# Edge loop of a four-layer graph network: one scatter product split into four, each on 32 columns of the array

## The chip, the cores and the metric

The kernel runs on one core of one Trainium2 chip. The metric is device time in microseconds (us) from launch to end; lower is better. A core has a matrix engine (TensorE, PE in the profile, with its weight loads listed apart as PEld), a vector engine (VectorE, DVE), a scalar engine (ScalarE, ACT), GpSimd (POOL) and SyncE (SP). Each runs its own list of instructions, and they wait for one another by semaphores. TensorE multiplies weights that were loaded into its array beforehand with a stream of columns, and adds the results up in PSUM, 8 banks of 128 partitions by 512 fp32 values.

## What is computed

Four graph layers one after the other on 1250 nodes with 512 features, each followed by a residual sum and a layer norm. The change lies in the second, a message layer over 21,250 edges. Cut to what matters:

```python
def _L1_gnn_ref(node_feats, edge_attrs, edge_feats, edge_index, ...):
    x0, x1 = _lin_irreps(x0, x1, W_up0, W_up1)
    h = edge_feats
    for W in (W_mlp1, W_mlp2, W_mlp3):
        h = SILU_2MOM * silu(h @ W / sqrt(W.shape[0]))
    w1, w2, w3, w4 = split(h @ W_mlp4 / sqrt(W_mlp4.shape[0]), 4)
    s0, s1 = x0[sender], x1[sender]
    y0, y1 = edge_attrs[:, 0:1], edge_attrs[:, 1:4]
    p1 = w1 * s0 * y0
    p2 = (w2 * s0)[:, :, None] * y1[:, None, :]
    p3 = w3[:, :, None] * s1 * y0[:, None, :]
    p4 = w4 * einsum('eum,em->eu', s1, y1) / SQRT3
    msg0 = segment_sum(concatenate([p1, p4], -1), receiver, 1250)
    msg1 = segment_sum(concatenate([p2, p3], 1), receiver, 1250)
    o0, o1 = _lin_irreps(msg0, msg1, W_out0, W_out1)
```

The two segment sums are what the changed product computes: for each edge 1024 message values are added to the row of its destination node.

## The kernel before

The edges have been sorted by destination into blocks of 125 nodes and padded. That gives G = 52 groups of 512 edges, each with destinations in one block only. The edge loop takes a group in GT = 4 steps of 128 edges, so it has 208 steps. It is written by hand for each engine, with two groups (`par` 0 and 1) to a turn of the hardware loop at L859.

For a step `k` the engines do this:

- TensorE, `tpw` (L847, L848): the last layer of the edge network, two products in the fp32r type of 128 x 512 into one of four banks (`tpw_bank`). The loop issues it three steps ahead of the step that it scatters.
- VectorE, `products` (L1604 to L1614): the messages `prod[:, k, :]`, 128 edges by 1152 values, and at L1606 `sel[:, k, :]`, the 128 x 125 matrix that holds a one where an edge's destination is that node. L1606 waits until the scatter four steps back is done (`s_scat_done`), since it overwrites its buffer.
- ScalarE: `first_term` (L1188), `times_y` (L1195 three times, then L1196, which makes `sely` out of `sel` by one of the edge's factors and lets the scatter go by `s_y_ok`).
- TensorE, `scat` (L852): two fp32 products with 128 edges as the contraction. The weights are the 125 columns of `sely` or `sel`, the stream is 512 columns of `prod`, and the result adds up over the four steps in two banks of PSUM, 125 partitions each. The banks alternate between the two groups, 2 and 3 or 4 and 5.

After each group VectorE adds the two banks into `acc` (`add_sums`, L1621) and prepares the low half of the hidden rows of a later group (`split_hidden`, L1627, after ScalarE's L1178). GpSimd fetches the sender rows of the group after next with four gathers (L597), after its copies L591 and L592, as soon as the group that used their buffers is read.

TensorE's list in the loop is strictly `tpw` three steps ahead, then `scat` of this step, then the next pair.

Of the kernel before, what the change touches and what calls it, by code (L numbers as in the profile page):

```python
# [10 lines left out]
NP, NB = 125, 10  # L11
KT = D // 128
EC = E // NP
GT = 4
# [51 lines left out]
def build(nc, a, out):  # L66
# [7 lines left out]
    with ctx:  # L74
# [39 lines left out]
        def at(off, shape, dt=f32):  # L114

            size = int(np.prod(shape[1:]))
            words = size if dt in (f32, f32r, i32, u32) else (size + 1) // 2
            assert off + words <= ARENA
            v = arena[:shape[0], off:off + words]
            if dt != f32:  # L120
                v = v.bitcast(dt)
            if len(shape) == 3:
                v = v.rearrange("p (a b) -> p a b", a=shape[1])
            if len(shape) == 4:
                v = v.rearrange("p (a b c) -> p a b c", a=shape[1], b=shape[2])
            return v

        PS = ctx.enter_context(nc.psum_tensor("PS", [128, 8, 512], f32))
# [81 lines left out]
        prod = at(14336, [128, GT, 9 * MUL])  # L210
# [411 lines left out]
        def _(pe):  # L622
            t = nc.tensor
# [123 lines left out]
            for b in range(NB):  # L747
# [3 lines left out]
                for j in range(NB):  # L751
                    ins = t.transpose(PS[:NP, 3 * (b % 2) + j // 4, (j % 4) * NP:(j % 4 + 1) * NP],
                                      cnt_f[:, b % 2, j * NP:(j + 1) * NP], ident[:NP, :NP])
# [38 lines left out]
            with pe.Fori(0, H // 2) as i:  # L792
                for par in range(2):
                    pe.wait_ge(s_hs_ok, i * 2 + (par + 1))
                    pe.wait_ge(s_head_free, i * 2 + (par + 1))
                    for sblk in range(NB):
                        pe.wait_ge(s_p_ok, i * (2 * NB) + (par * NB + sblk + 1))
                        for q in range(3):
                            n0, n1 = q * 512, min(N, (q + 1) * 512)
                            ins = t.matmul(PS[:, 3 * par + q, 0:n1 - n0], hs[:, sblk, par * C:par * C + 2 * C],  # L800
                                           wt[:, sblk % WR, n0:n1], start=(sblk == 0), stop=(sblk == NB - 1))
# [47 lines left out]

            def scat(par, k):  # L850
                for q, w in enumerate((sely, sel)):
                    ins = t.matmul(PS[:NP, 2 + 2 * par + q, :], w[:, k, :], prod[:, k, q * 512:(q + 1) * 512],  # L852
                                   start=(k == 0), stop=(k == GT - 1))
                ins.then_inc(s_scat_done, 1)
            pe.wait_ge(s_w4_ok, 2)
            pe.wait_ge(s_h3_ok, 1)
# [2 lines left out]
            with pe.Fori(0, G // 2) as i:  # L859
                for par in range(2):  # L860
                    pe.wait_ge(s_gsum_ok, i * 2 + (par + 1))
                    for k in range(GT):

                        if k == 1:
                            pe.wait_ge(s_h3_ok, i * 2 + (par + 2))
                        tpw((k + GT - 1) % GT, par if k == 0 else 1 - par)
                        pe.wait_ge(s_prod_ok, i * 8 + (4 * par + k + 1 + GT))
                        pe.wait_ge(s_y_ok, i * 8 + (4 * par + k + 1))
                        scat(par, k)
# [20 lines left out]
            for b in range(NB):  # L890
# [5 lines left out]
                for q in range(4):  # L896
                    pair = ((0, w_o0[:, 0, :]), (7, w_o0[:, 1, :])) if q == 0 else \
                           ((3 + q, w_o1[:, 0, :]), (q, w_o1[:, 1, :]))
                    for n, (c, w) in enumerate(pair):
                        ins = t.matmul(PS[:NP, 4 + b % 2, q * MUL:(q + 1) * MUL], msgT[:, b % 2, c * NP:(c + 1) * NP], w,  # L900
                                       start=(n == 0), stop=(n == 1))
# [16 lines left out]
            def agg_part(w, b0, k):  # L918

                for q in range(3):  # L920
                    n0, n1 = q * 512, min(N, (q + 1) * 512)
                    ins = t.matmul(PS[:, b0 + q, 0:n1 - n0], w, P50[:, k, n0:n1], start=(k == 0), stop=(k == NB - 1))  # L922
                return ins

            def x_feat(k, f):
                return x_sb[:, k, f * 128:(f + 1) * 128]

            for k in range(NB):
                pe.wait_ge(s_p2_ok, k + 1)
                for f in range(2):  # L930
                    ins = agg_part(x_feat(k, f), 3 * f, k)
# [10 lines left out]
            for q in range(3):  # L942
                n0, n1 = q * 512, min(N, (q + 1) * 512)
                ins = t.matmul(PS[:, q, 0:n1 - n0], ones[:NP, 0:128], Psum[:, n0:n1], start=True, stop=True)
# [29 lines left out]
            for b in range(NB + 1):  # L974
                if b < NB:
# [3 lines left out]
                    for k in range(KT):  # L979
                        ins = t.transpose(PS[:, 7, k * 128:k * 128 + NP], x_sb[:, b, k * 128:(k + 1) * 128], ident[:NP, :NP])  # L980
                    ins.then_inc(s_xt3_ps, 1)
                if b >= 1:
# [6 lines left out]
                    for k in range(KT):  # L989
                        ins = t.matmul(PS[:NP, 5 + c % 2, :], xT3[:, k, c * NP:(c + 1) * NP], w_l3[:, KT + k, :],  # L990
                                       start=(k == 0), stop=(k == KT - 1))
                    ins.then_inc(s_z_ps, 1)
            pe.wait_ge(s_z_cp, NB)
            for b in range(NB):
# [4 lines left out]
                for k in range(NB):  # L999
                    if b == 0:  # L1000
                        pe.wait_ge(s_p3_ok, k + 1)
                    ins = t.matmul(PS[:NP, b % 2, :], cnt50[:, k, b * NP:(b + 1) * NP], z_sb[:, k, :],  # L1002
                                   start=(k == 0), stop=(k == NB - 1))
# [784 lines left out]
```

## Time and profile before

| what | value |
|---|---|
| median of 3 runs | 2041.71 us (2039.19 to 2046.14) |
| profiled execution, its time | 2038.94 us |
| profiled execution, its span | 2036.9 us |
| granted TensorE clock, mean | 0.93 |
| busy over the whole span: PE, DVE, ACT | 83%, 79%, 44% |
| edge loop, first `tpw` to last `scat` | 872.4 to 1364.9 us, 492.5 us |

The span is the time from the first to the last instruction; what lies around it was 2.0 us in this execution. A step of the edge loop on TensorE is one row pair L847 and L848 and four records of L852 in the timeline. Each of the two fp32 products of `scat` appears as two weight loads and two matmuls, hence 832 records for 416 products. In the timeline the matmuls overlap on paper, since their ends are modelled with the way through the array. What tells the rate is the distance between starts.

### The profile page before, as it was taken

The numbers are of one execution on the slowest core, as the hardware profiler recorded it, in microseconds if no ns is written. First come the engines' busy times: TensorE is split into PE (matmuls) and PEld (weight loads), VectorE is DVE, ScalarE is ACT, GpSimd is POOL, SyncE is SP. The second block draws the span as 40 slices with busy tenths as digits, with TensorE's granted clock in tenths as the row PEclk, the third lists the DMA queues.
The fourth block names the chain that finished last, engine by engine and source line by source line (L and its number), as shares of the span: only waits on it lengthen the run. The fifth ranks groups of instructions, "written<-read, shape, count | busy, mean of one in ns | idle before, by whom it ended". The sixth has DMA issues, their size and how long they took to land.

```text
span 2036.9 us, 21846 instructions
## 1 busy us (share of the span) xinstructions
PE 1693.8 (83%) x5296; PEld 870.4 (43%) x5296; DVE 1607.7 (79%) x3252; ACT 895.4 (44%) x1833; POOL 527.2 (26%) x597
## 2 busy tenths in 40 slices
PE   2668888788387777479999999999598998999997
PEld 1445545533133333444444444457353443444443
DVE  9997899889899999789999999987665754762222
ACT  0112555666355454457777777763204423441100
POOL 4777870044000000045455555520000000002000
PEclk9788999988698899789999999998799999999999
DMA  5101000123210010154545454530010111111000
GB/s 166 10 6 8 6 5 1 36 101 110 103 39 35 32 42 0 56 150 140 151 135 155 133 154 136 153 74 1 25 42 21 62 62 62 58 56 52 0 25 25
DMA packets 66428, 133.78 MB, mean 66 GB/s; under 512 B 19156, under 2 KB 22752, under 8 KB 66385
## 3 DMA queue, kind: packets, MB, share of 16 engines
q1 hardware_dynamic: 40561, 70.33, 11.1%
q0 software_dynamic: 22080, 56.10, 10.3%
q10 hardware_dynamic: 3744, 6.82, 0.9%
q8 instruction: 22, 0.36, 0.1%
q14 instruction: 21, 0.17, 0.0%
HBM read 117.78 MB, written 15.24 MB: 65 GB/s over the span
## 4 chain that ended last, share of the span: by engine, by line
DVE 39%; PE 38%; issue 15%; DMA 4%; DVEq 3%; ACT 2%; SPq 0%; POOL 0%; ACTq 0%; POOLq 0%
PE PS L954 15%; DVE arena L1492 5%; PE PS L922 4%; PE PS L1002 4%; DVE arena L1608 4%; PE PS L738 3%; DVE arena L1488 3%; DVE arena L1353 3%; DVE arena L1604 3%; DVE arena L1611 2%; DVE arena L1614 2%; DVE arena L1352 2%; DVE arena L1383 2%; PE PS L998 2%; PE PS L990 2%
## 5 line engine op out<-in xcount | busy, mean ns | idle before, releaser
L852 PE MATMUL PS<-arena 128*125 128x512 f32 x832 | 397.1, 600 | 20.4 <-ACT arena L1196 20.3
L954 PE MATMUL PS<-arena 128*125 128x512 f32 x720 | 314.5, 600 | 12.2 <-ACT arena L1262 6.6
L1195 ACT ACTIVATE arena<-arena,gslot 128x128 f32<-128x128 f32 x624 | 204.4, 390 | 136.6 <-DVE arena L1608 129.0
L800 PE MATMUL PS<-arena 125*128 125x512 f32 (+1 forms) x480 | 196.3, 552 | 79.0 <-DVE arena L1492 78.9
L597 POOL DMA_INDIRECT arena<-xup,gidx x208 | 218.1, 1048 | 88.4 <-issue 50.0
L561 POOL DMA_INDIRECT recs<-arena x170 | 211.1, 1242 | 62.1 <-issue 47.7
L852 PEld LDWEIGHTS PS<-arena 128*125 128x125 f32 x832 | 152.2, 188 | 157.5 <-issue 101.3
L954 PEld LDWEIGHTS PS<-arena 128*125 128x125 f32 x720 | 136.8, 190 | 189.3 <-issue 189.3
L847 PE MATMUL PS<-w4r,h3r 128*128 128x512 f32 x211 | 168.2, 797 | 10.3 <-DVE h3r L1627 10.3
L800 PEld LDWEIGHTS PS<-arena 125*128 125x128 f32 x480 | 90.3, 199 | 185.1 <-DVE arena L1492 102.4
L1148 ACT ACTIVATE arena<-arena,c 125x1250 f32<-125x1250 f32 x80 | 107.0, 1337 | 137.6 <-DVE arena L1488 137.4
L738 PE MATMUL PS<-arena 128*125 128x512 bf16 (+1 forms) x624 | 128.5, 361 | 38.0 <-DVE arena L1383 37.8
L1488 DVE SCALAR_TENSOR_TENSOR arena<-arena,c 125x1250 f32<-125x1250 f32 x90 | 136.0, 1514 | 19.3 <-DMA arena<-uv_rows 17.1
L618 POOL CAST arena<-cnt_s 125x1250 f32<-125x1250 uint16 x10 | 12.6, 1303 | 513.7 <-PE PS L954 513.7
L591 POOL COPY gidx<-gld 128x4 uint32<-128x4 uint32 x52 | 9.7, 187 | 494.9 <-DMA gld<-recs 348.5
L1452 DVE CUSTOM_DVE_ANT_0 arena<-arena 125x1250 bf16<-125x1250 bf16 x80 | 111.2, 1454 | 10.1 <-DMA arena<-as_rows 7.8
L738 PEld LDWEIGHTS PS<-arena 128*125 128x125 bf16 x624 | 81.5, 145 | 88.0 <-DVE arena L1383 48.1
L1383 DVE TENSOR_SCALAR arena<-iota_src,pslot 128x1250 bf16<-128x1250 f16 x208 | 116.6, 581 | 0.0
L1492 DVE SCALAR_TENSOR_TENSOR arena<-arena,cnt_s 125x1250 f32<-125x1250 f32 x80 | 116.0, 1453 | 0.0
L1612 DVE TENSOR_TENSOR arena<-PS,arena 128x384 f32<-128x384 f32 x208 | 113.5, 546 | 0.0
L922 PE MATMUL PS<-arena,x_sb 125*128 125x512 f32 (+1 forms) x240 | 86.1, 520 | 19.3 <-DVE arena L1492 19.3
L771 PE MATMUL PS<-arena,w_m 16*128 16x512 f32 (+1 forms) x156 | 87.5, 690 | 17.5 <-ACT arena L1112 17.3
(235 smaller groups left out, 2905.9 us busy)
## 6 DMA issues: line engine op xcount, KB each, us to landing
arena<-in_spline_wT SPq DMA_DIRECT2D x16, 1024.0 KB, 5.3
arena<-h_rows SPq DMA_DIRECT2D x104, 128.0 KB, 3.4
arena<-uv_rows SPq DMA_DIRECT2D x18, 610.4 KB
h_rows<-arena ACTq DMA_DIRECT2D x26, 256.0 KB, 2.1
arena<-as_rows SPq DMA_DIRECT2D x8, 610.4 KB
arena<-xup,gidx POOLq DMA_INDIRECT x208, 4.2
recs<-arena POOLq DMA_INDIRECT x170, 2.6
x_sb<-in_x SPq DMA_DIRECT2D x1, 2500.0 KB
```

The source lines that it names most:

```text
L561: pool.indirect_dma_start(out=recs, out_offset=bass.IndirectOffsetOnAxis(stage_pos[:, sl, k:k + 1], 0), in_=stage_rec[:, sl, k, :], in_off ...
L597: pool.indirect_dma_start(out=ring[:, par * GT + k, :], out_offset=None, in_=xup, in_offset=bass.IndirectOffsetOnAxis(gidx[:, par, k:k + 1 ...
L738: ins = t.matmul(PS[:NP, 3 * par + q, 0:n1 - n0], oh_dst[:, par * GT + k, 0:NP], oh_src[:, par * GT + k, n0:n1], start=(k == 0), stop=(k = ...
L800: ins = t.matmul(PS[:, 3 * par + q, 0:n1 - n0], hs[:, sblk, par * C:par * C + 2 * C], wt[:, sblk % WR, n0:n1], start=(sblk == 0), stop=(sb ...
L847: t.matmul(PS[:, tpw_bank[k], :], h3r[:, par, cols], w4r[:, 0, :], start=True, stop=False)
L852: ins = t.matmul(PS[:NP, 2 + 2 * par + q, :], w[:, k, :], prod[:, k, q * 512:(q + 1) * 512], start=(k == 0), stop=(k == GT - 1))
L922: ins = t.matmul(PS[:, b0 + q, 0:n1 - n0], w, P50[:, k, n0:n1], start=(k == 0), stop=(k == NB - 1))
L954: ins = t.matmul(PS[:NP, b, :], basis[:, slot, (k * HB + b) * NP:(k * HB + b + 1) * NP], w_sp[:, slot, k * D:(k + 1) * D], start=(first an ...
L1195: A(pr[:, 4 + m, :], pr[:, 8, :], ACT.Copy, scale=y[:, 1 + m:2 + m])
L1383: ins = v.tensor_scalar(oh_src[:, par * GT + k, :], iota_src[:], pslot[:, par, k:k + 1], None, ALU.is_equal)
L1488: v.scalar_tensor_tensor(dst, U, cc, V, ALU.add, ALU.max).then_inc(ok, 1)
L1492: v.scalar_tensor_tensor(dst, e, 1.0, cm, ALU.min, ALU.mult).then_inc(ok, 1)
```

## The change

In `scat` the one product per half of the message becomes four. The first takes destination columns 0 to 31 of `sely` or `sel` as weights, the second 32 to 63, the third 64 to 95, the fourth 96 to 124, which is 29. Each names the 32 columns of the array that it is to use (`tile_position=(0, c0)`) and writes the 32 PSUM partitions of the same numbers. All four stream the same 128 x 512 block of `prod`. The semaphore is still raised once, by the last product. Nothing else is changed.

```diff
             def scat(par, k):
                 for q, w in enumerate((sely, sel)):
-                    ins = t.matmul(PS[:NP, 2 + 2 * par + q, :], w[:, k, :], prod[:, k, q * 512:(q + 1) * 512],
-                                   start=(k == 0), stop=(k == GT - 1))
+                    for c0 in range(0, NP, 32):
+                        c1 = min(NP, c0 + 32)
+                        ins = t.matmul(PS[c0:c1, 2 + 2 * par + q, :], w[:, k, c0:c1], prod[:, k, q * 512:(q + 1) * 512],
+                                       start=(k == 0), stop=(k == GT - 1), tile_position=(0, c0))
                 ins.then_inc(s_scat_done, 1)
```

TensorE's list around the first step of the loop, before: L847 and L848 are `tpw`, L852 is `scat`, the rest is the arithmetic of loop counters.

```order
405 L847 MATMUL PS<-w4r,h3r 128x512
406 L848 MATMUL PS<-w4r,h3r 128x512
407 L867 ISA
408 L868 REGISTER_ALU
409 L852 MATMUL PS<-arena 125x512 x2
```

The same list in the changed kernel, where the lines have moved by two, and `scat` is L854:

```order
409 L854 MATMUL PS<-arena 32x512 x3
410 L854 MATMUL PS<-arena 29x512
411 L854 MATMUL PS<-arena 32x512 x3
412 L854 MATMUL PS<-arena 29x512
413 L867 REGISTER_ALU
414 L847 MATMUL PS<-w4r,h3r 128x512
415 L848 MATMUL PS<-w4r,h3r 128x512
```

Two products between one `tpw` and the next have become eight, with the four that belong to one half of the message in a row; no instruction changes its place against another, and the lists of the other engines are as they were.

## Rows read from the trace of the kernel before

**Rows 1.** The page: busy time of the engines, share and instructions.

```profile
PE 1693.8 (83%) x5296; PEld 870.4 (43%) x5296; DVE 1607.7 (79%) x3252; ACT 895.4 (44%) x1833; POOL 527.2 (26%) x597
```

**Rows 2.** Busy us (instructions) by engine in the edge loop, granted clock, DMA.

```profile
core 0: us, PE busy (x) PEld busy (x) DVE busy (x) ACT busy (x) POOL busy (x), PEclk, DMA share, GB/s
872.00:1364.90 492.90, 472.10 (x1254) 233.58 (x1254) 459.73 (x1351) 346.95 (x1091) 243.94 (x310) 0.99 0.50 141
```

**Rows 3.** The chain that ended last, 1099 to 1109 us: shares by line.

```profile
by line: issue 22.9%; DVE arena L1608 19.7%; DVE arena L1611 13.0%; DVE arena L1604 12.1%; DVE arena L1614 10.3%; DVE h3r L1627 6.9%; DVE arena L1606 4.7%; DVE arena L1612 4.7%; DVEq L1617 3.5%; DVEq L1610 1.6%; DVEq L1603 0.8%; DVE arena L
```

**Rows 4.** L1627 in 1092 to 1113 us: count, ns min/median/max, first and last start.

```profile
L1627 DVE TENSOR_TENSOR h3r<-arena,h3r x3: 689/690/690, 1094.3 to 1112.9; 64x512 fp32r<-64x512 f32 x3
```

**Rows 5.** Timeline of PE: start us, us, what, count, [idle before <-releaser].

```profile
1100.68 1.95 PE L852 MATMUL PS<-arena 128*125 128x512 f32 x4 [0.41 <-ACT arena L1196]
1102.07 0.80 PE L847 MATMUL PS<-w4r,h3r 128*128 128x512 f32 x1
1102.70 0.39 PE L848 MATMUL PS<-w4r,h3r 128*128 128x512 f32 x1
1102.93 1.88 PE L852 MATMUL PS<-arena 128*125 128x512 f32 x4
1104.25 0.80 PE L847 MATMUL PS<-w4r,h3r 128*128 128x512 f32 x1
...
1108.62 0.79 PE L847 MATMUL PS<-w4r,h3r 128*128 128x512 f32 x1
```

**Rows 6.** Timeline of the weight loads of the same step.

```profile
1103.36 0.19 PEld L852 LDWEIGHTS PS<-arena 128*125 128x125 f32 x1 [0.24 <-issue]
1103.79 0.19 PEld L852 LDWEIGHTS PS<-arena 128*125 128x125 f32 x1 [0.24 <-issue]
1104.22 0.19 PEld L847 LDWEIGHTS PS<-w4r,h3r 128*128 128x128 f32 x1 [0.24 <-issue]
```

**Rows 7.** Waits in 880 to 1365 us: in total, times, longest.

```profile
POOL gidx L591 <- ACT arena L1196: 146.3, 50, 5.9
ACT arena L1195 <- DVE arena L1608: 129.0, 102, 4.0
...
PE PS L852 <- ACT arena L1196: 20.3, 48, 5.0
...
DVE arena L1621 <- PE PS L852: 2.6, 1, 2.6
```

**Rows 8.** Weight loads of L706, fp32 with 16 weight columns, one after another.

```profile
166.44 0.10 PEld L706 LDWEIGHTS PS<-arena,wa 128*16 128x16 f32 x1 [0.33 <-issue]
...
169.02 0.10 PEld L706 LDWEIGHTS PS<-arena,wa 128*16 128x16 f32 x1 [0.33 <-issue]
```

**Rows 9.** Engines' busy us and granted clock (sixth value) in the stretch of L706.

```profile
166.00:171.00 5.00, 5.00 (x17) 1.45 (x16) 2.95 (x5) 0.59 (x1) 3.80 (x5) 1.00 0.09 5
```

**Rows 10.** Timeline of PE from L706 (16 weight columns) to L658 (125).

```profile
170.02 1.11 PE L706 MATMUL PS<-arena,wa 128*16 128x226 f32 x5
171.07 1.15 PE L658 MATMUL PS<-wa,arena 128*125 128x16 f32 x9
```

**Rows 11.** The last of these by itself, its start and modelled length.

```profile
170.79 0.35 PE L706 MATMUL PS<-arena,wa 128*16 128x226 f32 x1
```

**Rows 12.** Timeline of PE at the start of the edge loop.

```profile
873.40 0.63 PE L847 MATMUL PS<-w4r,h3r 128*128 128x512 f32 x1
873.83 0.63 PE L848 MATMUL PS<-w4r,h3r 128*128 128x512 f32 x1
```

**Rows 13.** Engines' busy us and granted clock (sixth value) there.

```profile
873.00:876.00 3.00, 3.00 (x8) 1.96 (x6) 0.00 (x0) 0.00 (x0) 2.39 (x3) 0.53 0.56 178
```

**Rows 14.** The end of the loop: the last sum waits for the last scatter.

```profile
1365.05 1.22 DVE L1621 TENSOR_TENSOR arena<-PS,arena 125x1024 f32 x1 [3.12 <-PE PS L852]
```

## The prediction

> **What bounds the kernel now.** The page first: TensorE is busy for 83% of the span and VectorE for 79% [rows 1], a mean over stages that says nothing of this edit. So I read the stage it touches. In the edge loop TensorE is busy for 472 and VectorE for 460 of 493 us [rows 2], so two engines are nearly full. The chain of waits tells which of them sets the pace. It runs through VectorE's lines L1604 to L1627, with VectorE's own issue time between them, and the lines of `scat` and `tpw` are not in it [rows 3]. The list of waits agrees: TensorE waits for ScalarE (20.3 us, the end of a chain that starts on VectorE), and VectorE waited for a scatter only once, 2.6 us [rows 7]. The period of a group is VectorE's: L1627 comes once a group, and 1094.3 to 1112.9 are two periods, so 9.30 us, or 52 x 9.30 = 484 us for the loop [rows 4].
>
> TensorE's own need comes from the starts of its matmuls. When nothing holds it up a step takes 1104.25 - 1102.07 = 2.18 us [rows 5]. The weight loads inside `scat` start 0.43 us apart, 1103.36 and 1103.79 [rows 6], and there are four records to a step, two for each fp32 product. So `scat` streams for 4 x 0.43 = 1.72 us, and `tpw` takes the other 0.46 us. A group needs 4 x 2.18 = 8.72 us of TensorE. **The slack is 0.58 us a group**, 0.15 us a step. That is all that this edit may add before TensorE is the bound.
>
> **What the change removes and adds.** It removes 4 records of L852 a step and adds 16: eight products, each with two weight loads and two matmuls, if the split is as for all fp32 products here. The edit takes nothing from another engine. What one of the 16 costs is in the trace. L706 is an fp32 product with 16 weight columns; of its loads the first shown and the seventh start at 166.44 and 169.02, so 2.58 / 6 = 0.43 us apart [rows 8]. **A narrow product streams its 512 columns as slowly as a wide one.** What gets shorter is the weight load, 0.10 us against 0.19 [rows 6, 8], and that lies under the running matmul. Everything then hangs on how many of the 16 run at once, which no row shows, since no product of this kernel stands on other columns of the array than the first. The bounds, per step:
>
> - All in a row: 16 x 0.43 = 6.88 us.
> - Four at once throughout: 16 / 4 x 0.43 = 1.72 us, what `scat` takes now. Below it nothing is to be had: the 4 instructions of each tile must still stream one after another.
> - Between them, overlap only where neighbours in the list differ in tile. The list holds the two halves of one fp32 product next to each other, and both need the same 32 columns of the array. If matmuls start in the order of the list, the second half waits 0.43 us for the first, and the next tile's first half can start only behind it. The first half of each product then runs beside the second half of the one before. Eight products take 8 + 1 = 9 slots: 9 x 0.43 = 3.87 us.
>
> I take the last. The starts in the timeline follow the list everywhere that I looked [rows 5], and loads run ahead of a matmul by one slot and no further [rows 6], so I expect an engine that looks one step ahead, not one that sorts its work by tile.
>
> The Trainium skill, "TensorE: Matmul & The Clock Gate", section "Packing small matmuls — row/col tiling", says that matmuls on different tiles run at the same time, with four nanoseconds or so added per tile, and also that matmuls start and end strictly in program order. No run here shows either so far. Its sum for a pack counts one matmul per tile; an fp32 product has two. By its first sentence alone the result would be the second bound, by both together the third.
>
> **The switches.** Twice a step the array goes from its whole width to 32 columns and back. The trace has such a switch: L706 has 16 weight columns, L658 has 125. The last L706 starts at 170.79 [rows 11] and the first L658 at 171.07 [rows 10], 0.28 us; the L706 of that size start (170.79 - 170.02) / 4 = 0.19 us apart. So it costs 0.09 us; I take 0.1. The upper bound is the whole tail of the last matmul, 0.35 - 0.19 = 0.16 us [rows 11], and an uncovered wide load of 0.19 us [rows 6], 0.35 us together; the lower bound is nothing. The Trainium skill, "TensorEngine Tiling (Array Packing)", section "Key Properties", speaks against the change here: a change of tiling mode drains the engine. By the row a drain costs 0.1 us. Had the page meant the whole tail, the sum would be by the upper bound.
>
> **The sum.** Step: 3.87 (scatter) + 0.46 (`tpw`) + 2 x 0.1 (switches) = 4.53 us. Group: 18.1 us against VectorE's 9.30, so TensorE is the bound by far, and nothing covers the rest. VectorE, ScalarE and GpSimd then wait: `sel` and `prod` are kept for four steps and the sums alternate banks, so TensorE has its next operands in time. Loop: 208 x 4.53 = 942 us in place of 484, so **+458 us**. The start of the loop (before the first scatter) does not change. The tail, where L1621 waits 3.1 us for the last scatter [rows 14], grows by the 2.15 us that one scatter grows by, which the sum has in it. Span: 2036.9 + 458 = 2495 us. The median of the runs lies 4.8 us above the span of the profiled execution (2.8 above its own time, 2038.94), so I predict 2500 us.
>
> **The bounds of this case.** Switches at nothing: 4.33 x 208 = 901, so +417 and 2459 us. Switches at 0.35: 5.03 x 208 = 1046, so +562 and 2604. If half of the eight narrow loads that follow a load of the same tile are no longer covered, 4 x 0.10 x 208 = 83 us more, 2687.
>
> **Rivals.**
>
> 2. *All in a row.* The tiles share one stream. Step: 6.88 + 0.46 + 0.2 = 7.54 us, loop 1568, +1084, so 3126 us. For it: every narrow product in the trace is as long as a wide one [rows 8]. Against it: those all stand on the same columns, so they could not overlap.
> 3. *Faster.* The scatter ends sooner than 1.72 us, because the tiles' streams overlap even between the two halves. VectorE's 9.30 us remain the bound, and what TensorE can give back is what VectorE waits for it: 2.6 us in the loop [rows 7] and 3.1 at its end [rows 14], 6 us, so 2036. If all time in which VectorE isn't busy were such waits, it would be 493 - 460 = 33 us and 2009. It decides from a step below 2.18 us. Against it: rows 8 give no narrow matmul below 0.43 us.
> 4. *The clock.* At the start of the loop the granted clock is 0.53 in the mean, so mostly the lower level of 1.2 GHz, after TensorE sat idle, and an fp32r matmul there takes 0.43 us [rows 12, 13] instead of some 0.23. With all at the lower level the forecast's step is 2 x 4.33 + 0.2 = 8.86 us and the time about 3400. Against it: narrow matmuls in a row kept a granted clock of 1.00 [rows 9], and TensorE would be busier than before.
>
> **How the numbers follow.** Forecast 0.45, four at once 0.35, in a row 0.14, clock or another overlap 0.04, faster 0.02. The likeliest gives 2500, by itself 2459 to 2687. The range takes in the first two cases, 2048 to 2690, and leaves out in a row, the clock and faster: 0.2. A measurement of this kernel can tell about 0.3%, 6 us, from no change. Of the case of four at once a tenth may lie within that, so 0.04 for same; faster 0.02; slower 0.94.
>
> **What would show it.** In the profile after, the edge loop should take 950 us, its matmuls should come in starts 0.43 us apart with two records at each, and a step should be 4.5 us. VectorE's busy share in the loop should fall from 93% to about half, and the chain should run through TensorE. If the loads of the eight products start in fours within 0.1 us and a step is below 3 us, it is rival 1; if all 16 stand 0.43 apart, rival 2. The forecast is wrong if an fp32 product of 32 columns is not made of two halves, or if its halves do not stand side by side in what TensorE gets.

## The result, and the profile after

The changed kernel takes 2084.04 us (median of 4 runs, 2080.22 to 2086.16) against 2042.51 us (4 runs) for the kernel before: ratio 1.0201, 95% interval 1.0176 to 1.0226, 41.5 us slower. I had forecast 2500 us. The direction was right and the time lies inside the range, but the size was off by a factor of eleven: 458 us of loss forecast, 41.5 measured. What came is the first rival, four tiles at once throughout (2053 to 2157 us, most likely 2065). So the slower time does not bear out the forecast: its way to a loss, a scatter of 3.87 us, isn't there, and what makes the kernel slower is another term.

The page of the changed kernel, busy time by engine and the chain that ended last:

```profile
PE 1752.1 (84%) x7792; PEld 787.5 (38%) x7792; DVE 1608.7 (77%) x3252; ACT 895.4 (43%) x1833; POOL 526.5 (25%) x597
...
PE 60%; DVE 24%; issue 9%; DMA 4%; ACT 2%; DVEq 1%; SPq 0%; POOL 0%; ACTq 0%; POOLq 0%
```

Against [rows 1] TensorE has 2496 more matmul records, 12 for each of 208 steps, as forecast, and only 58 us more busy time. The edge loop from the first `tpw` to the last `scat` (busy us and records of PE, PEld, DVE, ACT, POOL, then the granted clock), and the shares by line of the chain in 1109 to 1119 us:

```profile
878.40:1411.90 533.50, 528.07 (x3750) 148.62 (x3750) 458.46 (x1350) 346.77 (x1090) 243.60 (x310) 0.99 0.46 130
```

```profile
by line: PE PS L854 73.9%; PE PS L847 17.1%; PE PS L848 9.4%
```

The loop takes 533.5 us in place of 492.5: the whole loss, 41.0 us, is in it. VectorE does the same work in it, 458 us against 460 [rows 2], and the chain, which ran through VectorE alone [rows 3], now runs through TensorE alone. (The loop starts 6 us later in this execution. The edit has no part ahead of it, and the medians differ by 41.5 us, so I give that no cause; executions of the kernel before lie up to 7 us apart.)

The timeline of PE in the steady loop (start us, us, what, how many records), which answers to [rows 5]:

```profile
1120.28 0.50 PE L847 MATMUL PS<-w4r,h3r 128*128 128x512 f32 x1
1120.61 0.40 PE L848 MATMUL PS<-w4r,h3r 128*128 128x512 f32 x1
1120.94 1.92 PE L854 MATMUL PS<-arena 128*32 128x512 f32 x16
1122.79 0.50 PE L847 MATMUL PS<-w4r,h3r 128*128 128x512 f32 x1
...
1130.33 0.50 PE L847 MATMUL PS<-w4r,h3r 128*128 128x512 f32 x1
```

Sixteen records stand in 1.85 us, from 1120.94 to the next `tpw` at 1122.79. One record alone streams for 0.43 us, so 16 in a row would be 6.88. The weight loads of the same stretch, which answer to [rows 6]:

```profile
1120.93 0.15 PEld L854 LDWEIGHTS PS<-arena 128*32 128x32 f32 x8 [0.36 <-issue]
1121.39 0.12 PEld L854 LDWEIGHTS PS<-arena 128*32 128x32 f32 x4 [0.30 <-issue]
1121.82 0.12 PEld L854 LDWEIGHTS PS<-arena 128*32 128x32 f32 x4 [0.30 <-issue]
1122.79 0.19 PEld L847 LDWEIGHTS PS<-w4r,h3r 128*128 128x128 f32 x1 [0.84 <-issue]
```

Eight loads go at once, two for each tile (one to work with, one ahead), then four and four at distances of 0.43 to 0.46 us. That is the sign that I had named for rival 1. All four tiles stream side by side, and a tile's second half does not hold up the next tile. Four records of 0.43 us to a tile are 1.72 us, as before.

So `scat` costs what it did, and the loss lies at its edges. A step is (1130.33 - 1120.28) / 4 = 2.51 us, 0.33 more than 2.18. From `scat` to `tpw` it is 1.85 us instead of 1.72, 0.13 more; from `tpw` to `scat` 1120.94 - 1120.28 = 0.66 instead of 0.46, 0.20 more.

These two pieces are not the two directions, since the first load after a change falls into the piece behind it. The rows allow a finer split. The second round of narrow loads comes 1121.39 - 1120.93 = 0.46 us after the first, and the third 0.43 after that: 0.03 us are the first narrow load, which no running matmul covers. The other 0.10 of the 0.13 pass between the end of the last narrow record and the load of L847. Then L847 starts 0.33 us ahead of L848, and L848 0.33 ahead of `scat`, where a product of this kind takes 0.23 between wide neighbours (shown below in the run on the slack). The first 0.10 is the wide load of L847, now uncovered (the next load starts 0.10 behind it); the second passes between the end of L848 and the narrow loads. So, by this reading of starts, each change of shape has a pause of 0.10 us and behind it a first load that nothing covers: 0.10 + 0.03 = 0.13 us from wide to narrow, 0.10 + 0.10 = 0.20 from narrow back to wide.

The load of L847 shows the change of shape. In [rows 6] it starts 0.24 us after the load before it ends, under a running matmul. Here the load engine stands idle for 0.84 us and starts at 1122.79, with the matmul record that it belongs to. A group now takes 1130.33 - 1120.28 = 10.05 us of TensorE against 9.30 of VectorE, and 52 x 0.75 = 39 us of the 41 follow. The list of waits in 880 to 1405 us (in total, times, longest) has what answers to the last two lines of [rows 7]:

```profile
DVE arena L1623 <- PE PS L854: 60.8, 51, 3.2
...
PE PS L854 <- ACT arena L1198: 5.4, 1, 5.4
```

VectorE's sum at the end of a group waited once for a scatter before; now it waits in 51 of 52 groups, 1.2 us each. TensorE's 48 waits for ScalarE, 20.3 us, have shrunk to one of 5.4 us.

### The profile page after: what moved, and what is told of

It reads as the page before. It is cut to its first block, busy times and chain, and to the rows that moved or that the text cites. A ratio compares the mean times of both kernels' runs of the same rounds, so it can differ in the third digit from the quotient of the medians.

```text
span 2084.0 us, 26838 instructions
## 1 busy us (share of the span) xinstructions
PE 1752.1 (84%) x7792; PEld 787.5 (38%) x7792; DVE 1608.7 (77%) x3252; ACT 895.4 (43%) x1833; POOL 526.5 (25%) x597
## 4 chain that ended last, share of the span: by engine, by line
PE 60%; DVE 24%; issue 9%; DMA 4%; ACT 2%; DVEq 1%; SPq 0%; POOL 0%; ACTq 0%; POOLq 0%
PE PS L854 19%; PE PS L956 15%; DVE arena L1494 5%; PE PS L847 4%; PE PS L924 4%; PE PS L1004 4%; DVE arena L1355 3%; DVE arena L1490 3%; PE PS L738 3%; PE PS L848 2%; DVE arena L1385 2%; DVE arena L1354 2%; PE PS L1000 2%; PE PS L992 2%; DVE arena L1506 2%
## 5 line engine op out<-in xcount | busy, mean ns | idle before, releaser
L854 PE MATMUL PS<-arena 128*32 128x512 f32 (+1 forms) x3328 | 401.5, 600 | 5.4 <-ACT arena L1198 5.4
L956 PE MATMUL PS<-arena 128*125 128x512 f32 x720 | 314.4, 600 | 12.2 <-ACT arena L1264 6.6
L956 PEld LDWEIGHTS PS<-arena 128*125 128x125 f32 x720 | 136.8, 190 | 189.3 <-issue 189.3
L854 PEld LDWEIGHTS PS<-arena 128*32 128x32 f32 (+1 forms) x3328 | 84.4, 109 | 208.5 <-issue 192.7
L1623 DVE TENSOR_TENSOR arena<-PS,arena 125x1024 f32 x52 | 63.7, 1224 | 66.2 <-PE PS L854 66.2
L847 PE MATMUL PS<-w4r,h3r 128*128 128x512 f32 x211 | 105.8, 501 | 10.2 <-DVE h3r L1629 10.2
L847 PEld LDWEIGHTS PS<-w4r,h3r 128*128 128x128 f32 x211 | 39.9, 189 | 185.5 <-issue 185.2
```

Of the source, the lines that this page charges most:

```text
L847: t.matmul(PS[:, tpw_bank[k], :], h3r[:, par, cols], w4r[:, 0, :], start=True, stop=False)
L854: ins = t.matmul(PS[c0:c1, 2 + 2 * par + q, :], w[:, k, c0:c1], prod[:, k, q * 512:(q + 1) * 512], start=(k == 0), stop=(k == GT - 1), til ...
L956: ins = t.matmul(PS[:NP, b, :], basis[:, slot, (k * HB + b) * NP:(k * HB + b + 1) * NP], w_sp[:, slot, k * D:(k + 1) * D], start=(first an ...
```

## Experiments

Two theories after the result. **Shape**: the tiles cost nothing, and going to the narrow shape and back costs 0.33 us of TensorE a step, of which VectorE's pace had hidden 0.15. **Record**: each of the 12 more records costs 0.0275 us of issue, which is also 0.33. The runs also test whether the tiles overlap fully, and how far the engine sees ahead. Differences below are each against the kernel before as it ran beside them.

**One tile of the four.**

```diff
-                    for c0 in range(0, NP, 32):
+                    for c0 in (0,):
```

> Only the product on the first 32 columns is left, so the sums of the other 93 destination nodes of a block are left out. Four matmul records a step instead of 16, all on one tile. If the four tiles of the changed kernel run fully beside one another and the extra 0.33 us of a step is the price of going to the narrow shape and back, a step stays at 2.51 us and the time at 2084 us. If the 0.33 us is paid per record (12 more records, 0.0275 us each), the step is back at 2.18 us, VectorE is the bound again and the time is 2042 us. If the tiles overlap only in part, the step falls below 2.4 us, and the time below 2070 us.

Measured: 2080.49 us against 2044.27, ratio 1.0186 (1.0169 to 1.0203), 36 us slower.

```profile
1121.50 1.90 PE L854 MATMUL PS<-arena 128*32 128x512 f32 x4
1123.33 0.50 PE L847 MATMUL PS<-w4r,h3r 128*128 128x512 f32 x1
...
1125.83 0.50 PE L847 MATMUL PS<-w4r,h3r 128*128 128x512 f32 x1
```

With a quarter of the records the scatter still takes 1123.33 - 1121.50 = 1.83 us and the step 2.50. So the other three tiles are almost free: 0.02 us a step, or the 4 to 5 us between 36 and 41.5. The record theory, which wanted 2042 us, is out.

**The tiles one by one.**

```diff
-                for q, w in enumerate((sely, sel)):
-                    for c0 in range(0, NP, 32):
-                        c1 = min(NP, c0 + 32)
+                for c0 in range(0, NP, 32):
+                    c1 = min(NP, c0 + 32)
+                    for q, w in enumerate((sely, sel)):
```

> The same eight products a step, in another order: both halves of the message on the first 32 columns, then both on the next, and so on. Four matmul records in a row now want the same tile. If each tile has a line of its own for at least four waiting instructions, nothing changes: step 2.51 us, 2084 us. If the engine starts matmuls in the order of the list (what the prediction took), the step is over 4.5 us and the time over 2500 us. If it looks ahead by two records only, a tile blocks for 0.86 us before the next one starts: 3 x 0.86 us more a step, 2.6 us, and the time is over 2600 us.

Measured: 2088.0 us against 2044.27, ratio 1.0221 (1.0204 to 1.0239). The weight loads:

```profile
1121.64 0.17 PEld L854 LDWEIGHTS PS<-arena 128*32 128x32 f32 x8 [0.36 <-issue]
1122.09 0.15 PEld L854 LDWEIGHTS PS<-arena 128*32 128x32 f32 x4 [0.28 <-issue]
1122.52 0.15 PEld L854 LDWEIGHTS PS<-arena 128*32 128x32 f32 x4 [0.28 <-issue]
```

Four records in a row want the same tile here, and still eight loads go first and then four and four. Whose they are can be told by shape, since the fourth tile alone has 29 columns. The first eight loads by shape (1121.64 to 1121.82 us), and the matmuls that run in 1121.72 to 1121.82:

```profile
L854 PEld LDWEIGHTS PS<-arena 128*32 128x32 f32 x6 | 0.2, 108 | 0.4 <-issue 0.4
L854 PEld LDWEIGHTS PS<-arena 128*29 128x29 f32 x2 | 0.1, 106 | 0.0
```

```profile
L854 PE MATMUL PS<-arena 128*32 128x512 f32 x3 | 0.6, 617 | 0.0
L854 PE MATMUL PS<-arena 128*29 128x512 f32 x1 | 0.6, 615 | 0.0
```

In the order of the list the fourth tile's records are the last four of the sixteen. Two of its loads are among the first eight, and one of its matmuls runs among the first four. So a record that waits for its tile does not stop those behind it, at least 12 records deep (the fourth tile's first is the thirteenth). Whether each tile has a queue of its own or one queue is searched, the times can't tell. The step is 2.53 us instead of 2.51.

**Two tiles of 64 columns.**

```diff
-                    for c0 in range(0, NP, 32):
-                        c1 = min(NP, c0 + 32)
+                    for c0 in range(0, NP, 64):
+                        c1 = min(NP, c0 + 64)
```

> Two products on 64 and 61 columns in place of four on 32: 8 matmul records a step. If the price is that of the change of shape, twice a step, it is there in full: step 2.51 us, 2084 us. If it is paid per record, 4 more records cost 0.11 us, less than TensorE's slack of 0.15 us, and the time is 2042 to 2046 us.

Measured: 2086.75 us, ratio 1.0211 (1.0191 to 1.023).

```profile
1121.96 0.50 PE L847 MATMUL PS<-w4r,h3r 128*128 128x512 f32 x1
1122.30 0.40 PE L848 MATMUL PS<-w4r,h3r 128*128 128x512 f32 x1
1122.62 1.94 PE L854 MATMUL PS<-arena 128*64 128x512 f32 x8
1124.49 0.50 PE L847 MATMUL PS<-w4r,h3r 128*128 128x512 f32 x1
```

Half the records, and the same price: step 2.53 us, with the same 0.66 us ahead of the scatter. The price is that of leaving the wide shape and coming back, the same for 64 columns as for 32.

**Every second step.**

```diff
+                    wd = 32 if k % 2 else 128
-                    for c0 in range(0, NP, 32):
-                        c1 = min(NP, c0 + 32)
+                    for c0 in range(0, NP, wd):
+                        c1 = min(NP, c0 + wd)
```

> The four narrow products only in steps 1 and 3 of a group, the one wide product in steps 0 and 2. If the loss comes from 0.33 us in each changed step, a group needs 2 x 2.18 + 2 x 2.51 = 9.38 us of TensorE against VectorE's 9.30, so some 4 us more than before plus what two nearly equal engines lose to one another: 2044 to 2058 us. If the loss were in proportion to the changed steps, it would be half of 41 us: 2063 us.

Measured: 2050.03 us against 2044.27, ratio 1.0028 (1.0015 to 1.0041), 5.8 us.

```profile
1120.95 0.50 PE L847 MATMUL PS<-w4r,h3r 128*128 128x512 f32 x1
...
1125.66 0.50 PE L847 MATMUL PS<-w4r,h3r 128*128 128x512 f32 x1
```

Two steps take 4.71 us and a group 9.42, so 52 x 0.12 = 6 us. Half the changes of shape cost a seventh of the loss, since most of them fit into TensorE's slack.

**The slack by itself, without tiles.** The kernel before, with one short product more in each step:

```diff
+                t.matmul(PS[:, tpw_bank[k], :], h3r[:, par, cols], w4r[:, 1, :], start=False, stop=False)
                 t.matmul(PS[:, tpw_bank[k], :], h3r[:, par, cols], w4r[:, 1, :], start=False, stop=True).then_inc(s_tpw_ps, 1)
```

> The kernel before, all wide, with the second product of tpw (L848) issued twice, so that the message weights are off in their low part: 0.22 us more of TensorE a step, no tiles. It tests the slack of 0.15 us a step. Step 2.40 us, group 9.60 us against 9.30: 208 x 2.40 - 484 = 15 us more, and some more from two nearly equal engines: 2057 to 2070 us. If the slack is larger than 0.22 us, 2043 us.

Measured: 2061.12 us against 2041.03, ratio 1.0097 (1.0076 to 1.0117), 20 us.

```profile
1120.92 0.79 PE L847 MATMUL PS<-w4r,h3r 128*128 128x512 f32 x1
1121.56 0.40 PE L848 MATMUL PS<-w4r,h3r 128*128 128x512 f32 x1
1121.79 0.39 PE L849 MATMUL PS<-w4r,h3r 128*128 128x512 f32 x1
1122.02 1.88 PE L853 MATMUL PS<-arena 128*125 128x512 f32 x4
1123.34 0.79 PE L847 MATMUL PS<-w4r,h3r 128*128 128x512 f32 x1
```

The step is 2.42 us here, and one short product between wide neighbours takes 0.23 (L848, L849 and L853 start 0.23 apart). 0.23 us more of TensorE's time a step cost 20 us, where 208 x 0.23 = 48 would be due without slack. The rule "52 x (TensorE's group - 9.30)" gives 18 to 20 us for this run, 6 for the one with every second step (5.8 measured) and 39 for the change (41.5 measured). The 2 us or so that are left may be what two nearly equal engines lose to each other; no run shows it.

**A loop without a change of shape.** To have `tpw` on column tiles too I replaced its two fp32r products by one fp32 product of the same rows. That is slower, so three kernels: all wide, only the scatter narrow, both narrow.

```diff
-                t.matmul(PS[:, tpw_bank[k], :], h3r[:, par, cols], w4r[:, 0, :], start=True, stop=False)
-                t.matmul(PS[:, tpw_bank[k], :], h3r[:, par, cols], w4r[:, 1, :], start=False, stop=True).then_inc(s_tpw_ps, 1)
+                for c0 in range(0, 128, 32):
+                    ins = t.matmul(PS[c0:c0 + 32, tpw_bank[k], :], h3r[:, par, k * 128 + c0:k * 128 + c0 + 32].bitcast(f32), w_m4,
+                                   start=True, stop=True, tile_position=(0, c0))
+                ins.then_inc(s_tpw_ps, 1)
```

The diff is that of the third; the first two have one product in place of the loop.

> The scatter as before, wide. The two fp32r products of tpw are replaced by one fp32 product of the same rows with the unrounded weights, which can be split into column tiles. All wide, no change of shape. It is the base for the next two. Two records at 0.43 us in place of 0.46 us: step 1.72 + 0.86 = 2.58 us, TensorE is the bound, 208 x 2.58 - 484 = 53 us more than before: 2097 us.

> The same fp32 tpw, wide, with the scatter of the changed kernel: two changes of shape a step. If a pair of them costs 0.33 us whatever stands on either side: step 2.91 us, 605 - 484 = 121 us more than before: 2165 us, 69 us above the all-wide one. If the 0.33 us belonged to the fp32r products (a short product after which nothing covers a load), it would be 2097 to 2110 us.

> The fp32 tpw too in four products on 32 columns, so that the whole loop stays in one shape: 24 records a step, none wide. If the loss comes from the changes of shape, it is gone: step 2.58 us, 2097 us, as with all wide. If narrow tiles cost something of their own (more records, the end of a pack), it stays at 2.8 us or more and 2140 us or more.

Measured against 2041.03 us: all wide 2095.1 (ratio 1.0261, 1.0232 to 1.0289), scatter narrow 2162.25 (1.0598, 1.0571 to 1.0625), both narrow 2096.17 (1.0274, 1.0253 to 1.0295). The timeline of the second, then of the third:

```profile
1121.40 1.92 PE L853 MATMUL PS<-arena 128*32 128x512 f32 x16
1123.25 1.13 PE L847 MATMUL PS<-arena,h3r 128*128 128x512 f32 x2
1124.31 1.92 PE L853 MATMUL PS<-arena 128*32 128x512 f32 x16
```

```profile
1119.68 1.90 PE L856 MATMUL PS<-arena 128*32 128x512 f32 x16
1121.40 1.04 PE L848 MATMUL PS<-arena,h3r 128*32 128x512 f32 x8
1122.26 1.90 PE L856 MATMUL PS<-arena 128*32 128x512 f32 x16
```

This decides it. With two changes of shape a step is 1124.31 - 1121.40 = 2.91 us, with none 1122.26 - 1119.68 = 2.58, in the kernel with nothing but narrow products, the same as with nothing but wide ones to 1 us of the whole time. The price is 67 us / 208 = 0.32 us a step. The two pieces are those of the changed kernel: 1123.25 - 1121.40 = 1.85 in place of 1.72 from `scat` to `tpw`, 1124.31 - 1123.25 = 1.06 in place of 0.86 from `tpw` to `scat`. It has nothing to do with the fp32r type.

**Scatters in pairs.** The changed kernel, with the changes of shape halved by order alone:

```diff
-                    for k in range(GT):
-                        if k == 1:
-                            pe.wait_ge(s_h3_ok, i * 2 + (par + 2))
+                    for k in (0, 2):
                         tpw((k + GT - 1) % GT, par if k == 0 else 1 - par)
+                        if k == 0:
+                            pe.wait_ge(s_h3_ok, i * 2 + (par + 2))
                         pe.wait_ge(s_prod_ok, i * 8 + (4 * par + k + 1 + GT))
+                        tpw(k, 1 - par)
                         pe.wait_ge(s_y_ok, i * 8 + (4 * par + k + 1))
                         scat(par, k)
+                        pe.wait_ge(s_prod_ok, i * 8 + (4 * par + k + 2 + GT))
+                        pe.wait_ge(s_y_ok, i * 8 + (4 * par + k + 2))
+                        scat(par, k + 1)
```

> The changed kernel with TensorE's list in pairs: tpw of two steps, then the narrow scatters of two steps, so one change of shape and back for two steps. Saved against the changed kernel: 2 x 0.33 = 0.66 us a group, so 9.38 us and 2050 us, if nothing else waits. The second tpw of a pair now needs the hidden rows of the next group right after the first step of this one, 0.7 us or so of TensorE's time a group: 10.1 us and 2085 us at most. Below 2075 us it says that the price is one of the changes of shape; at 2084 us or above it says nothing.

Measured: 2047.52 us against 2041.09, ratio 1.0027 (1.0014 to 1.004). Of the 41.5 us 35 are back, with all 3328 narrow records in place.

```profile
1119.91 0.50 PE L847 MATMUL PS<-w4r,h3r 128*128 128x512 f32 x1
...
1121.05 3.64 PE L854 MATMUL PS<-arena 128*32 128x512 f32 x32
1124.61 0.50 PE L847 MATMUL PS<-w4r,h3r 128*128 128x512 f32 x1
```

Two steps take 4.70 us, a group 9.40: TensorE and VectorE are level. The wait for the hidden rows, which I feared, doesn't show.

**Is VectorE the bound of the kernel before?** Then taking work off it must gain. L1627 (0.69 us a group) goes to GpSimd, at first in the kernel before and in the changed one as it stands:

```diff
-                        if k == 0:
-                            split_hidden(1 - par, i * 2 + (4 - par))
...
+            def split_low(par, n, n_gath):
+                for k in range(GT):
+                    pool.wait_ge(s_gath[(1 - par) * GT + k], n_gath)
+                pool.wait_ge(s_h3hi_ok, n)
+                pool.nop(nofuse=True)
+                pool.tensor_tensor(h3r[HID:128, par, :], h3[HID:128, par, :], h3r[HID:128, par, :].bitcast(f32), ALU.subtract)\
+                    .then_inc(s_h3_ok, 1)
...
```

> The kernel before, all wide, with the 50 subtractions of L1627 in the loop (0.69 us each) moved from VectorE to GpSimd, ahead of the gathers of the same group. If VectorE's 9.30 us a group is what bounds the kernel before, and TensorE comes next with 8.72 us, the group falls to 8.72 to 8.9 us: 52 x 0.4 to 0.58 us less, 2012 to 2022 us. If GpSimd's later gathers become the wait, or VectorE was not the bound, 2035 to 2045 us.

> The same move in the changed kernel. There TensorE needs 10.05 us a group, so relief for VectorE should bring nothing: 2080 to 2085 us. If the two engines slow each other down (the loss of the change is partly VectorE's), it falls below 2075 us.

Measured: 2099.1 us (ratio 1.0285, 1.0271 to 1.0299) and 2096.41 us (1.0268, 1.0252 to 1.0283) against 2041.09. Both missed what I expected. The waits of the first in 900 to 1350 us:

```profile
POOL h3r L610 <- DMA arena<-xup,gidx: 106.8, 34, 4.3
ACT arena L1201 <- DMA arena<-xup,gidx: 103.0, 43, 3.5
```

In this form GpSimd waits until its own gathers have landed (the loop over `s_gath`) before it subtracts, 3.1 us each time. The next gathers start that much later, and ScalarE waits for them. A new wait took the place of the old bound, and the two runs say nothing on the question. Nearly equal times with wide and narrow scatters show only that TensorE did not bound these two.

The same again without that wait, and in the kernel before alone. Into a second buffer ScalarE writes zero for rows 0 to 63 and the rounded values for rows 64 to 127, and GpSimd subtracts that buffer over all 128 partitions. So one operation makes rows 0 to 63 and the low halves in rows 64 to 127.

```diff
-                A(h3r[:, par, :], h3[:, par, :], ACT.Copy).then_inc(s_h3hi_ok, 1)
+                A(h3m[:, par, :], h3[:, par, :], ACT.Copy, scale=low[:, 0:1]).then_inc(s_h3hi_ok, 1)
...
+                pool.wait_ge(s_h3hi_ok, n)
+                pool.nop(nofuse=True)
+                pool.tensor_tensor(h3r[:, par, :], h3[:, par, :], h3m[:, par, :].bitcast(f32), ALU.subtract)\
+                    .then_inc(s_h3_ok, 1)
...
```

> Again the kernel before, all wide, with the subtractions of L1627 on GpSimd, but in a form over all 128 partitions (ScalarE writes zero over the upper 64 rows), so that GpSimd need not wait until its earlier gathers have landed, which cost 107 us of waiting in the run before this one. VectorE then needs some 8.6 us a group, TensorE 8.72. If VectorE's 9.30 us bounded the kernel before and the gathers, 1.1 us later than before, are still in time: 52 x 0.3 to 0.58 us less, 2012 to 2026 us. If the gathers are late by their new delay: 2040 to 2060 us.

Measured: 2030.6 us against 2043.62, ratio 0.9939 (0.9924 to 0.9955), 13 us faster than the kernel before, which the changed one trails by 41.5 us. That is less than the 16 us (52 x 0.3) at least that I had named. Its L611 (count, ns min/median/max, first and last start):

```profile
L611 POOL TENSOR_TENSOR h3r<-arena x3: 1272/1282/1282, 1107.5 to 1125.6; 128x512 fp32r<-128x512 f32 x3
```

The group takes (1125.6 - 1107.5) / 2 = 9.05 us instead of 9.30, and 52 x 0.25 = 13 us. Work taken off VectorE gains, which together with the chain in [rows 3] and the run on the slack says that VectorE was the bound before. TensorE's 8.72 us is not reached, and the trace says why. The chain in 1110 to 1128 us, by line, then VectorE's L1616 (L1604 in the kernel before) without and with GpSimd's subtraction beside it:

```profile
by line: issue 24.4%; DVE arena L1616 18.2%; DVE arena L1620 18.0%; DVE arena L1623 11.5%; DVE arena L1626 10.8%; DVEq L1629 5.5%; DVE arena L1618 5.1%; DVE arena L1624 4.1%; DVEq L1622 1.6%; DVE arena L1633 0.9%; DVEq L1645 0.7%; DVEq L163
```

```profile
1124.37 0.34 DVE L1616 SCALAR_TENSOR_TENSOR arena<-arena,gslot 128x128 f32<-128x128 f32 x1
...
1125.60 1.28 POOL L611 TENSOR_TENSOR h3r<-arena 128x512 fp32r<-128x512 f32 x1 [1.78 <-ACT arena L1190]
...
1126.08 0.95 DVE L1616 SCALAR_TENSOR_TENSOR arena<-arena,gslot 128x128 f32<-128x128 f32 x1
```

The chain still runs through VectorE. Once a group its L1616 takes 0.95 us in place of 0.34 while L611 runs; over the loop L1616 takes 494 ns in the mean, against 341 for L1604 in the kernel before. That is 4 x 0.153 = 0.61 us a group, most of the 0.69 that had been taken off. So the move relieved VectorE far less than its expectation reckoned. That the group is shorter by 0.25 us and not by the 0.08 that these two leave, these rows do not explain.

## Why the prediction was wrong, point by point

- **What bounds the kernel, and the slack: right.** VectorE's 9.30 us a group against TensorE's 8.72, so 0.15 us a step is free. The doubled short product (20 us for 0.23 us a step) bears out the slack, and the moved subtraction (13 us gained) fits VectorE as the one that sets the pace.
- **Number and length of the records: right.** 16 a step, each streaming 0.43 us.
- **How many run at once: wrong, and this is the step that failed.** I put "the second half waits 0.43 us for the first, and the next tile's first half can start only behind it", so nine slots and 3.87 us. Measured are four slots, 1.72 us. The rows I rested it on show one shape only, where every record wants the same columns. There an engine that keeps the list's order and one that sorts by tile look the same; I took rows that could not tell the two apart as a sign for one of them. The tile-by-tile run shows that a waiting record holds up nobody else. This one term is 208 x 2.15 = 447 us.
- **The Trainium skill.** "TensorE: Matmul & The Clock Gate", section "Packing small matmuls — row/col tiling", was right in the sentence that matmuls on different tiles run at once: 16 records in 1.85 us. Its small extra per tile is of the size seen here, 0.02 us a step for three more tiles. Its other sentence, that matmuls start strictly in program order, does not hold here: in the tile-by-tile kernel a matmul of the fourth tile, thirteenth in the list or later, runs with the first of the other three. The measurement decides.
- **The switches: right in kind, low in size.** I took 0.1 us each from one place, [rows 10, 11]; measured are 0.13 from wide to narrow and 0.20 back, together 0.33, where I had put 0.35 at most for each. The 0.09 us of that row run up to the record of L658, with which its own load starts, so they are the pause alone, and the pause was right: 0.10 us each way. What I left out of the sum is the first load behind each change, which nothing covers, 0.03 and 0.10 us; I had it in the upper bound only. In rival 1 this is most of the miss: with 0.33 in place of 0.2 its 2.38 us a step become 2.51, and its 2053 us become 2080. Its likeliest 2065 had another 12 us or so from TensorE's waits for ScalarE, which did not stay (one of 5.4 us). The Trainium skill, "TensorEngine Tiling (Array Packing)", section "Key Properties", says that changing the mode drains the engine. The trace agrees, with 0.33 us for a pair, and the run with both products narrow shows that a change of tile alone costs nothing.
- **The chances.** Forecast 0.45, four at once 0.35. No row spoke for either, and the page that I cited had a sentence for each. I let a picture of the engine's inside carry the point forecast. That the range still took in the measured time is owed to the rival in it, not to the forecast.

## What to carry to other kernels

Splitting a product that already fills the array into column tiles gains nothing: the tiles run beside one another and together take as long as the one. What it costs is each change between the whole array and tiles, here 0.33 us for a pair: a pause each way, and a first load each way that nothing covers. Keep all products of a loop in one shape, or collect those of one shape, and weigh what is left against TensorE's slack to the engine that sets the pace. Tiles should pay where several narrow products that now run one after another can stand side by side: four took 0.02 us a step more than one. Of the order in the list two kinds were run, half by half and tile by tile, and they lie 0.02 us a step apart.

## What I had not expected of the hardware

- Four fp32 streams over all 128 rows run at once at the full rate: 1.85 us for 16 records that take 0.43 us each, at a granted clock of 0.99 over the loop.
- Four records in a row for one tile don't hold up the twelve behind them (step 2.53 us against 2.51).
- Coming back to the wide shape costs more (0.20 us, 0.10 of it the uncovered wide load) than leaving it (0.13 us), and the pair costs about the same for 64 columns as for 32 (step 2.53 and 2.51 us).
- GpSimd's subtraction of 128 x 512 values takes 1.28 us beside a busy VectorE, and the gathers that it delays are still in time. But the VectorE instruction beside it, of 128 x 128 values, takes 0.95 us instead of 0.34.
